# A gated MLP with top-k selection: the first two pairs of tiles ordered anew, the down weights' low parts on GpSimd

## The reference

```python
xn = layernorm(x)
s = silu(xn @ w_gate.T)                 # 1376 values per token
s[the 688 of smallest |s| in a token] = 0
s = (s * (xn @ w_up.T)) @ w_down.T
q = ternary(weight)                     # 1 / 0 / -1 by 0.7 * mean|row|
g = silu(xn @ q.T + bias)
x = x + s * g
```

## Time and profile before

| what | us |
|---|---|
| median of 3 runs (lowest, highest) | 653.42 (652.19, 653.88) |
| profiled execution, first to last instruction (its span; no other time of it is shown) | 650.9 |
| TensorE busy, share of the span | 611.2 (94%) |
| VectorE | 481.2 (74%) |
| ScalarE | 330.7 (51%) |
| GpSimd | 168.5 (26%) |

### The profile page before, as it was taken

How to read it: one execution, slowest core, us unless ns; L and a number is a source line. 1 busy time by engine, 2 the same in 40 slices (tenths; PEclk the granted TensorE clock), 3 DMA queues, 4 the chain that set the end, 5 groups by cost and what they waited for, 6 DMA issues and landing times. The chain is left out here.

```text
span 650.9 us, 8590 instructions
## 1 busy us (share of the span) xinstructions
PE 611.2 (94%) x2764; PEld 445.3 (68%) x2764; DVE 481.2 (74%) x923; ACT 330.7 (51%) x551; POOL 168.5 (26%) x296
## 2 busy tenths in 40 slices
PE   4797899999999999999999999999799999999775
PEld 3686778888888888888888888877654444444332
DVE  6898797888788788788788879677486555555455
ACT  5769367347528518726744842847333343343320
POOL 1000001001001100200100100489875555543234
PEclk9999899999999999999999999999799999999887
DMA  8811000110020020020011001460300000000015
GB/s 294 327 45 66 0 2 0 38 62 1 1 97 0 0 97 0 0 90 7 0 35 62 0 1 66 130 237 1 68 0 1 0 1 0 2 1 1 0 64 194
DMA packets 17181, 32.34 MB, mean 50 GB/s; under 512 B 3224, under 2 KB 3736, under 8 KB 17152
## 3 DMA queue, kind: packets, MB, share of 16 engines
q1 hardware_dynamic: 17152, 31.99, 14.3%
HBM read 24.63 MB, written 7.35 MB: 49 GB/s over the span
## 5 line engine op out<-in xcount | busy, mean ns | idle before, releaser
L775 DVE TENSOR_SCALAR_CACHE_REDUCE junk_d<-k_buf,cand 128x1376 int8<-128x1376 f32 x56 | 91.9, 1641 | 0.3
L599 ACT ACTIVATE junk_a<-k_buf,cand 128x1376 int8<-128x1376 f32 x56 | 80.5, 1437 | 0.6
L580 ACT ACTIVATE s_buf<-ps_a 128x1376 f32<-128x1376 f32 x16 | 21.1, 1320 | 108.5 <-PE ps_a L1045 106.1
L1075 PE MATMUL ps_a<-wd_hi,zt_hi 128*128 128x512 f32 (+1 forms) x176 | 71.8, 408 | 1.0 <-issue 0.8
L1075 PE MATMUL ps_a<-wd_hi,zt_lo 128*128 128x512 f32 (+1 forms) x176 | 69.3, 394 | 0.0
L1075 PE MATMUL ps_a<-wd_lo,zt_hi 128*128 128x512 f32 (+1 forms) x176 | 68.8, 391 | 0.0
L1777 PE MATMUL ps_b<-arena,xt 128*128 128x512 f32 x128 | 63.6, 611 | 0.0
L493 POOL TENSOR_TENSOR rstd<-var_eps,expo 128x2 f32<-128x2 f32 x8 | 5.6, 706 | 208.1 <-DVE var_eps L716 208.1
L501 POOL TENSOR_TENSOR xres<-xres,gate 128x512 f32<-128x512 f32 x12 | 22.4, 1868 | 141.7 <-DVE gate L901 141.7
L1045 PE MATMUL ps_a<-wg_hi,xt_hi 128*128 128x512 f32 (+1 forms) x192 | 52.8, 384 | 2.2 <-DVE xt_lo L704 2.2
L1045 PE MATMUL ps_b<-wu_hi,xt_hi 128*128 128x512 f32 (+1 forms) x192 | 52.5, 382 | 0.0
(11 more groups left out here) (222 smaller groups left out, 1282.9 us busy)
## 6 DMA issues: line engine op xcount, KB each, us to landing
xin<-in_x SPq DMA_DIRECT2D x8, 512.0 KB, 4.1
xres<-in_x SPq DMA_DIRECT2D x8, 512.0 KB, 3.4
out<-arena SPq DMA_DIRECT2D x16, 256.0 KB, 2.0
x_scratch<-xres SPq DMA_DIRECT2D x6, 514.0 KB, 4.1
arena<-x_scratch SPq DMA_DIRECT2D x3, 1028.0 KB, 12.2
m_buf<-in_wd_t SPq DMA_DIRECT2D x3, 512.0 KB, 9.1
m_buf<-in_wg_t SPq DMA_DIRECT2D x2, 688.0 KB, 5.4
k_buf<-in_wg_t SPq DMA_DIRECT2D x2, 688.0 KB, 8.0
```

What stands on the lines that cost most here:

```text
L580: act.activation(s_buf[:, t, :], ps_a[:].rearrange("p a n -> p (a n)")[:, 0:INNER], ACT.Silu).then_inc(s_ready, 1)
L599: act.activation(junk_a[:], k_buf[:, 1, :], ACT.Sign, bias=c, scale=-1.0, accum_out=below[:, 1:2]).then_inc(act_step, 1)
L775: dve.tensor_scalar(junk_d[:], k_buf[:, 0, :], c, -float(DROP), ALU.is_lt, ALU.add, accum_out=e).then_inc(cnt_dve, 1)
L1075: last = pe.matmul(ps_a[:, t, :], zs, ws[0:rows, c, :], start=(c == 0 and n == 0), stop=(c == CHUNKS - 1 and n == 2))
```

## The change

SyncE: x of pair 0 is loaded tile by tile, tile 0 first, then the first weights, then tile 1. The staging buffers are used by a new list: units 0 to 5 have a buffer each (the sixth, `wide`, lies over `gate2` and `bias_b`), units 8 and 12 use `xres`. The bias is loaded later, when six low parts are done.

GpSimd: the root is taken for tile 0 and tile 1 apart, and `down_low` makes the low parts of units 8 to 13. Waits on these use a semaphore of their own, `wd_l`.

ScalarE: a silu of one column at the start; the high parts and x's high parts in a new order; the ternary sums after the keys of tile 0; units 8 to 11 right behind them, 12 and 13 between search steps; in pair 1 the first three blocks of z before the silu of tile 1.

VectorE: tile 0 of x is normalised alone, tile 1 after the second low part; the ternary thresholds in two instructions instead of eight, the values after the first search step; no low parts of down weights; in pair 1 the product, the first low parts of z and two search steps are placed ahead (`begun`).

TensorE: 18 transposes of the identity before the first of x and 6 after it; the first projection waits for each part separately; x of tile 1 is transposed inside it; the ternary transposes stand behind the gate projection of tile 1 (two) and inside the up projection (two); flags stand inside projections (in the loop too), and have a 128-column operand of ones; pair 1 is written out.

The diff, cut to its core:

```diff
             def slot_of(u):
-                return u % 4 if u < N_GU else (0, 1, 3, 4)[(u - N_GU) % 4]
+                return (0, 1, 2, 3, 4, 6, 0, 1, 5, 4, 0, 1, 5, 0)[u]
...
-                       s_buf[:, 1, :])[slot_of(u)]
+                buf = (m_buf[:, 0, :], m_buf[:, 1, :], k_buf[:, 0, :], k_buf[:, 1, :], s_buf[:, 1, :],
+                       xres[:].rearrange("p t h -> p (t h)"), wide[:])[slot_of(u)]
...
-                load_x(xin, x_in, 0)
-                for u in range(len(units)):
+                sp.dma_start(xin[:, 0, :], x[0:P, :]).then_inc(x_first, 16)
+                sp.dma_start(slot_ap(0), units[0][0]).then_inc(w_in[slot_of(0)], 16)
+                sp.dma_start(xin[:, 1, :], x[P:2 * P, :]).then_inc(x_in, 16)
+                for u in range(1, len(units)):
                     prev = [v for v in range(u) if slot_of(v) == slot_of(u)]
                     if prev:
-                        sp.wait_ge(w_lo, prev[-1] + 1)
+                        if prev[-1] < N_GU:
+                            sp.wait_ge(w_lo, prev[-1] + 1)
+                        else:
+                            sp.wait_ge(wd_l, prev[-1] - N_GU + 1)
                         sp.wait_ge(w_hi, prev[-1] + 1)
                     sp.dma_start(slot_ap(u), units[u][0]).then_inc(w_in[slot_of(u)], 16)
                     if u == N_GU - 1:
@@ -429,6 +446,8 @@
                             sp.dma_start(stage[:, 2 * t:2 * t + 2, :],
                                          tern_w[2 * P * t:2 * P * (t + 1), :].rearrange("(k p) n -> p k n", p=P)
                                          ).then_inc(tern_in, 16)
+                    if u == N_GU:
+                        sp.wait_ge(w_lo, 6)
                         sp.dma_start(bias_b[:], ffn_bias.partition_broadcast(P)).then_inc(bias_in, 16)
                         sp.wait_ge(xt_psum, 2)
...
+                def down_low(u):
+                    pool.wait_ge(w_hi, u + 1)
+                    pool.tensor_tensor(units[u][3], slot_ap(u), units[u][2].bitcast(F32),
+                                       ALU.subtract).then_inc(wd_l, 1)
+                pool.wait_ge(ve_first, 1)
+                pool.tensor_tensor(rstd[:, 0:1], var_eps[:, 0:1], expo[:, 0:1], ALU.pow).then_inc(rs_first, 1)
+                pool.wait_ge(ln_ve, 1)
+                pool.tensor_tensor(rstd[:, 1:2], var_eps[:, 1:2], expo[:, 0:1], ALU.pow).then_inc(ln_rs, 1)
+                for u in range(N_GU, N_GU + 4):
+                    down_low(u)
                 root(1)
+                for u in range(N_GU + 4, len(units)):
+                    down_low(u)
                 with pool.Fori(1, PAIRS - 1) as p:
...
+                    if isinstance(p, int) and p == 1:
+                        act.wait_ge(q_done, t + 1)
...
-                for u in range(2):
+                def ternary_mags():
+                    act.wait_ge(tern_in, 32)
+                    for k in range(KH):
+                        if k:
+                            act.wait_ge(t_mag, k)
+                        act.activation(junk_a[:, 0:HID], stage[:, k, :],
+                                       ACT.Abs, accum_out=mags[:, k:k + 1]).then_inc(t_mag, 1)
+                act.wait_ge(c_const, 4)
+                act.activation(side[:], one[:], ACT.Silu).then_inc(silu_in, 1)
+                split_hi(0)
+                xt_high(0, 0)
+                split_hi(1)
+                split_hi(2)
+                split_hi(3)
+                xt_high(0, 1)
+                for u in range(4, N_GU - 1):
                     split_hi(u)
-                for t in range(2):
-                    xt_high(0, t)
-                for u in range(2, N_GU):
...
                 def silu_keys(p, t, wait_free):
                     act.wait_ge(gate_done, 2 * p + t + 1)
-                    if not wait_free:
-                        act.wait_ge(w_lo, N_GU + 4 if t else N_GU)
                     if wait_free:
                         act.wait_ge(mask_ready, 2 * p + t - 1)
+                    elif t:
+                        act.wait_ge(wd_l, 2)
+                    else:
+                        act.wait_ge(w_lo, 4)
                     act.activation(s_buf[:, t, :], ps_a[:].rearrange("p a n -> p (a n)")[:, 0:INNER],
...
+                        split_hi(N_GU - 1)
                     act.wait_ge(s_ready, 2 * p + t + 1)
                     act.activation(k_buf[:, t, :], s_buf[:, t, :], ACT.Abs,
...
+                def pair(p, back, ahead, first=False, begun=0):
                     for t in range(2):
                         silu_keys(p, t, not first)
+                        if t == 0:
+                            for i in range(begun):
+                                zt_high(p, i)
                         if first and t == 0:
+                            ternary_mags()
+                            for u in range(N_GU, N_GU + 4):
+                                split_hi(u)
...
                             for k in range(2):
-                                tern_copy(k)
-                            for u in range(N_GU, len(units)):
-                                split_hi(u)
-                            for k in range(2, KH):
                                 tern_copy(k)
                     search_start(p)
                     for n in range(STEPS):
...
+                            if n == 0:
+                                for k in range(2, KH):
+                                    tern_copy(k)
+                            if n in (2, 3):
+                                xt_high(p + 1, n - 2)
+                            if n in (1, 4):
+                                split_hi(N_GU + 4 + n // 4)
                             if n == 5:
                                 at_most_first(p)
                             continue
-                        if back and n < 5:
+                        if back and not begun and n < 5:
...
-                norm_stats(0)
-                norm_apply(0)
+                for t, loaded, made in ((0, x_first, ve_first), (1, x_in, ln_ve)):
+                    dve.wait_ge(loaded, 16)
+                    dve.bn_stats(stats[:, t, :], xin[:, t, :]).then_inc(ln_st, 1)
+                    dve.wait_ge(ln_st, t + 1)
+                    settled(dve, dve_passed)
+                    dve.bn_aggr(mv[:, t, :], stats[:, t, :]).then_inc(ln_mv, 1)
+                    dve.wait_ge(ln_mv, t + 1)
+                    dve.tensor_scalar(var_eps[:, t:t + 1], mv[:, t, 1:2], EPS, None, ALU.add).then_inc(made, 1)
+                    if t == 0:
+                        dve.wait_ge(rs_first, 1)
+                        dve.tensor_scalar(xin[:, 0, :], xin[:, 0, :], mv[:, 0, 0:1], rstd[:, 0:1],
+                                          ALU.subtract, ALU.mult).then_inc(xn_ready, 1)
                 split_lo(0)
-                for t in range(2):
-                    xt_low(0, t)
-                for u in range(1, N_GU):
+                xt_low(0, 0)
+                split_lo(1)
+                dve.wait_ge(ln_rs, 1)
+                dve.tensor_scalar(xin[:, 1, :], xin[:, 1, :], mv[:, 1, 0:1], rstd[:, 1:2],
+                                  ALU.subtract, ALU.mult).then_inc(xn_ready, 1)
+                split_lo(2)
...
-                    dve.wait_ge(t_mag, k + 1)
-                    dve.tensor_scalar(thr[:, k:k + 1], mags[:, k:k + 1], 1.0 / HID, TERNARY,
-                                      ALU.mult, ALU.mult).then_inc(t_thr, 1)
-                    dve.wait_ge(t_thr, 2 * k + 1)
-                    dve.tensor_scalar(thr_neg[:, k:k + 1], thr[:, k:k + 1], -1.0, None,
-                                      ALU.mult).then_inc(t_thr, 1)
+                def ternary_thresholds():
+                    dve.wait_ge(t_mag, KH)
+                    dve.tensor_scalar(thr, mags, 1.0 / HID, TERNARY, ALU.mult, ALU.mult).then_inc(t_thr, 1)
+                    dve.wait_ge(t_thr, 1)
+                    dve.tensor_scalar(thr_neg, thr, -1.0, None, ALU.mult).then_inc(t_thr, 1)
+                    dve.wait_ge(t_thr, 2)
...
@@ -910,30 +984,38 @@
                 def first_pair():
                     bracket(0)
                     halve(0, 0)
+                    ternary_thresholds()
+                    for k in range(KH):
+                        ternary_values(k)
+                    product(0, 0)
                     halve(0, 1)
-                    product(0, 0)
-                    for u in range(N_GU, N_GU + 4):
-                        split_lo(u)
                     halve(0, 2)
                     norm_stats(1)
                     halve(0, 3)
                     norm_apply(1)
-                    for u in range(N_GU + 4, len(units)):
-                        split_lo(u)
                     product(0, 1)
...
+                    xt_low(1, 0)
                     halve(0, 5)
-                    xt_low(1, 0)
+                    xt_low(1, 1)
                     halve(0, 6)
-                    xt_low(1, 1)
                     dve.wait_ge(bias_in, 16)
```

(56 more changed lines are left out.)

126 lines of the change are left out of this document (76 added, 50 removed).

## The result

The changed kernel takes 645.96 us in the median of four runs (645.43 to 647.21), the kernel before on the same chip 652.81 us (651.88 to 653.88): a ratio of 0.9898, with an interval of 0.9885 to 0.9912. The forecast was 648.1 us. The profiled span went from 650.9 to 643.6 us.

A forecast was written before the change was run, and what follows sets the result against it. Before pair 2 TensorE and VectorE wait for each other in turn; later pairs are bound by TensorE. Pair 2 starts 5.3 us earlier, flags and pair 2 count 0: span 650.9 to 645.6, plus 2.5 gives 648.1 us; range 638.5 to 652.5.

The forecast's parts named there:

- Start: Pair 0: first matmuls at 7.5 us instead of 10.49, up projection of tile 0 ending at about 24.7 instead of 27.1.
- Ternary values: Pair 0: four GpSimd collisions of 2.2 us delay VectorE's ternary values from 31.2 to 39.9; TensorE stands 7.6 us.
- rival B: GpSimd's down-weight subtractions take over 2.2 us: from 3.5 each, slower than the kernel before; at 5.3, 660.5 us; chance 0.05.
- Back to VectorE's chain: From ternary values to pair 2: 6.8 us of low parts leave VectorE, first flag's wait 0.5 us, pair 2 at 110.5.
- Pair 2: Pair 2: pair 1's choices come 3 us later against TensorE; counted as nothing, bound 0 to 2 us.
- Flags: Fourteen loop flags, 128 columns: between -0.1 and +0.25 us each, -1.5 to +3.5 in all; counted as 0.
- Rival A: GpSimd's operations don't land between the ternary values, which end at 31.2: shift 14 us, time 639.5; chance 0.26 with part cases.
- The page weighed: VectorE excludes GpSimd only in two-port mode or with two SBUF inputs, leaving search passes untouched; otherwise 1 to 3 us longer.

The follow-up runs named there:

- Run 4: Changed kernel with each of GpSimd's first four low-part subtractions made twice: 650.23 us, ratio 0.9935 to the kernel before.
- Run 7: Changed kernel with the loops' flags behind the fourth group of their projection, not the second: 646.13 us, ratio 0.9896 to the kernel before.
- run 6: Changed kernel with the flag sums in the old form (flag column stationary, one output row), places kept: 647.42 us, ratio 0.9906 to the kernel before.
- Run 1: Changed kernel with GpSimd's low parts of the down weights started only after the four ternary values: 645.37 us, ratio 0.9868 to the kernel before.
- run 3: Changed kernel with GpSimd writing zeros instead of the first four subtractions, those low parts left out: 637.76 us, ratio 0.9742 to the kernel before.
- run 10: Changed kernel with ten GpSimd subtractions as 512-column halves, each started beside a chosen VectorE instruction, none beside norm_apply: 637.29 us, ratio 0.9769 to the kernel before.
- run 8: Changed kernel with four GpSimd subtractions placed, waiting for chosen VectorE instructions, unit 12 ungated: 641.39 us, ratio 0.9832 to the kernel before.

## Why the prediction was right

The direction, the place and the mechanism held, and the time was 2.1 us off. Some of that closeness is luck: against the forecast pair 2 starts 1.7 us earlier and lasts 1.6 longer, the flags of the later pairs give 0.8, and 1.2 come behind the start of pair 7, which nothing forecast and which is within the noise of single traces; in the changed kernel's second trace pair 2 starts at 110.65, beside the forecast 110.5.

- *Start:* first matmuls at 7.36 (forecast 7.5), at the high level of the clock; the up projection of tile 0 ends at 24.4 (24.7). Keys ready at 21.8, not 22.6: all behind it 0.8 us earlier.
- *Ternary values:* they end at 38.16 (39.9), that is 16.4 us behind the keys where I had 17.3. Four collisions, as forecast; 8.2 us in place of 8.7. GpSimd's own work in one, from VectorE's release to its end, is about 2.26 us, so the size of 2.2 was right. TensorE stood 6.1 us (7.6) and came back at the low clock. Run 4 confirms the turns; rival B (over 3.5 us for one) is out.
- *Back to VectorE's chain:* up projection of tile 1 to 49.85 (50.6), gate projection of pair 1 at 55.5 (56.2), first flag at 67.19 (68.0) with a wait of 0.21 (0.5), no slow groups behind it. Pair 2 at 108.84 (110.5): 0.8 of the difference is the earlier keys, the rest a wait for `gate` at the end of pair 1 that didn't come.
- *Pair 2:* counted at nothing with a bound of 2 us; it is 1.6 us longer than before. This was the term nearest to wrong. 0.9 of it stands before a flag, and is a collision again: GpSimd's residual sum begins at 108.87 and holds the second small instruction of VectorE's choice (1.10 us, where it takes 0.23 in fourteen of the sixteen tiles), and the flag waits for this choice. Before, the residual sum at this point held a pass for the other tile, and the flag came without a wait. Set beside pair 3, which is 1.8 us shorter, matmul start by matmul start, the late flags cost 1.3 us with their longer steps, and 0.4 come at zt_lo, 0.17 of it idle. Run 7 shows that moving the flags doesn't win it.
- *Flags:* counted at nothing, bounds -0.1 to +0.25 each: -0.10 by run 6, at the lower bound, in pairs 3 to 6. Their 0.8 us offset half of what pair 2 lost.
- *Rival A's size* was right, but not its condition. I had put 639.5 us on the ternary values being undisturbed. Run 1 had that and took 645.4. The prediction missed that the small instructions of the search, with two operands in SBUF, collide as well: in the changed kernel GpSimd's fifth subtraction, at 50.28, shows it (the addition beside it 1.13 us in place of 0.15). Runs 3 and 10 (637.8 and 637.3 us) show what is there when nothing, or almost nothing, collides.
- *The page weighed:* search passes, products and statistics were left alone, as the Trainium skill ("SBUF — State Buffer", "SBUF: two separate sides") states, and its condition "with two SBUF inputs" names the small additions too; I had read it with only wide instructions in mind. It also names a two-port mode, which a `TENSOR_SCALAR` can enter by the same page: `norm_apply` in run 8 (3.07 us for 1.00) and the first instruction of each ternary value (2.6 for 0.48) were held, at the faster rate worked out above.

## What to carry to other kernels

Work moved from VectorE to GpSimd isn't free where the two meet: list what kind of VectorE instruction stands beside it, small ones too, and not only how busy the engine is. By run 10 a GpSimd pass that reads SBUF belongs beside VectorE's search passes, statistics and passes with an operand in PSUM, cut to fit them and started by a semaphore that VectorE raises there; against run 3, where GpSimd only writes (0.9742), the same subtractions cost some 10 us in one place (0.9898) and about 2 in another (0.9769), each to 1 us or so. And a wait that is taken away should be followed on: in run 1 the next wait, of 6.2 us, had the same cause.

## What the runs showed of the hardware that I had not expected

- A VectorE addition of one column per partition, 0.15 us by itself, was held for 2.32 us by a GpSimd subtraction of 1024 columns, while a pass of 1376 columns with one operand kept its 1.64.
- A GpSimd write of 1024 columns without a read, 0.96 us, lengthened a VectorE `TENSOR_SCALAR` of 0.48 us by 0.13 us at most, while a subtraction held one for 2.1.
- 128 columns of weights for a flag sum, though loaded in 188 ns and not 81, made the step 0.10 us shorter, where TensorE didn't wait for the flag.
